# Sums behind the second products, and a group's scatters out of its fourth slot, in a three-attention decoder layer with a routed mixture

## The reference

```python
x = _layernorm(x + _L0_attn_ref(x, ...))            # "ret": scores * decay mask, no softmax, normalised, gated
x = _layernorm(x + _L0_xattn_ref(x, ctx_1024, ...)) # "cross": softmax over the context's rows
h = layernorm(x + self_attention(x), g1, b1)        # "self": causal softmax
probs = softmax(h @ wg); topv, topi = top_k(probs, 2); topv = topv / topv.sum(-1)
h1 = gelu(einsum('bsd,edf->ebsf', h, w1) + bb1)     # 8 experts, 128 -> 512 -> 128
y = einsum('ebsf,efd->ebsd', h1, w2) + bb2
x = _layernorm(x + layernorm(h + moe, g2, b2))      # moe: each row's two experts by their weights
```

## Time and profile before

| | |
|---|---|
| median of three runs | 1313.32 us (1298.87 to 1319.24) |
| profiled execution | 1299.05 us, of which the span from the first to the last instruction is 1297.8 |
| busy in the span | PE 82%, PEld 59%, DVE 67%, ACT 64%, POOL 70% |
| mean granted TensorE clock | 0.893 of full speed |
| longest parts of the chain that ended last | PE 42%, issue 14%, DVE 14%, POOL 14%, ACT 10% |

### The profile page before, as it was taken

The page is one execution under the profiler, slowest core; times in us unless marked ns, Lnnn a source line. Parts: engine busy times, 40 slices in busy tenths (PEclk is TensorE's granted clock), DMA queues, the critical chain, the costliest instruction groups (busy, mean ns, idle before and its releaser), DMA issues.

```text
span 1297.8 us, 45997 instructions
## 1 busy us (share of the span) xinstructions
PE 1063.3 (82%) x17677; PEld 761.5 (59%) x17677; DVE 865.0 (67%) x2370; ACT 824.6 (64%) x1884; POOL 911.1 (70%) x859
## 2 busy tenths in 40 slices
PE   5888888788998888888988888847788799999552
PEld 2555555554555555555555555637777789999310
DVE  4677776766888777777767776545454466666485
ACT  2355554678999887777777776414445466666377
POOL 3788888866766657777777776766666656667596
PEclk9999898987999999989888997657889999999886
DMA  5465332221233223222222221111212233332453
GB/s 158 129 185 147 88 86 63 63 60 54 75 85 85 80 66 85 68 67 68 79 65 65 77 77 35 52 34 43 61 54 63 66 88 98 99 100 78 143 164 97
DMA packets 132181, 108.61 MB, mean 84 GB/s; under 512 B 19563, under 2 KB 122476, under 8 KB 131932
## 3 DMA queue, kind: packets, MB, share of 16 engines
q1 hardware_dynamic: 123548, 88.29, 24.9%
q0 software_dynamic: 8416, 17.38, 3.8%
HBM read 41.58 MB, written 26.75 MB: 53 GB/s over the span
## 4 chain that ended last, share of the span: by engine, by line
PE 42%; issue 14%; DVE 14%; POOL 14%; ACT 10%; DMA 3%; another core or an unknown queue 2%; DVEq 1%; SPq 1%; POOLq 0%; ACTq 0%
PE bank L1211 7%; PE bank L1202 7%; POOL Plo L769 7%; PE bank L547 3%; PE bank L612 3%; PE bank L550 3%; DVE P L841 2%; DMA xrow<-block_rows 2%; PE bank L487 2%; DVE st L873 2%; DVE mx L817 2%; PE bank L450 2%; PE bank L517 2%; PE bank L510 2%
## 5 line engine op out<-in xcount | busy, mean ns | idle before, releaser
L769 POOL TENSOR_TENSOR Plo<-P 128x1024 f16<-128x1024 f32 x192 | 364.7, 1901 | 162.2 <-ACT P L726 136.1
L1254 POOL DMA_INDIRECT expert_rows<-yo,ix x135 | 173.0, 1281 | 103.3 <-DVE ix L1248 73.4
L1225 ACT ACTIVATE G<-bank,we 128x128 f32<-128x128 f32 x540 | 154.9, 372 | 103.6 <-PE bank L1202 85.3
L817 DVE TENSOR_REDUCE mx<-bank 128x16 f16<-128x1024 f32 x128 | 156.7, 1225 | 42.3 <-PE bank L465 33.2
L687 ACT ACTIVATE Kz<-kh,col 128x512 f16<-128x512 f16 x256 | 167.1, 717 | 0.1
L1211 PE MATMUL bank<-we,G 128*128 128x128 f32 x1080 | 151.5, 286 | 16.7 <-ACT G L1225 12.6
L787 POOL DMA_INDIRECT block_rows<-xs,slots x128 | 132.6, 1036 | 39.8 <-issue 38.4
L510 PE MATMUL bank<-Vh,P 64*128 64x17 f16 (+1 forms) x3072 | 148.6, 170 | 10.2 <-issue 10.2
L726 ACT ACTIVATE P<-bank 128x1024 f32<-128x1024 f32 x128 | 131.1, 1024 | 39.7 <-PE bank L487 38.2
L510 PEld LDWEIGHTS bank<-Vh,P 64*128 64x128 bf16 x3072 | 125.6, 94 | 49.8 <-issue 37.2
L511 PE MATMUL bank<-Vh,Plo 64*128 64x17 f16 (+1 forms) x3072 | 145.9, 168 | 9.4 <-issue 9.3
(11 more groups left out here) (187 smaller groups left out, 2169.5 us busy)
## 6 DMA issues: line engine op xcount, KB each, us to landing
Qz<-qh SPq DMA_DIRECT2D x192, 64.0 KB, 2.0
Kst<-kh SPq DMA_DIRECT2D x192, 64.0 KB
xrow<-block_rows SPq DMA_DIRECT2D x135, 65.0 KB
y_t<-expert_rows SPq DMA_DIRECT2D x16, 512.0 KB, 4.1
Qz<-ql SPq DMA_DIRECT2D x96, 64.0 KB, 2.0
Kst<-kl SPq DMA_DIRECT2D x96, 64.0 KB
xT<-xt SPq DMA_DIRECT2D x16, 256.0 KB, 3.1
xs<-x SPq DMA_DIRECT2D x16, 256.0 KB, 4.1
```

The source lines that it names most:

```text
L769: pool.tensor_tensor(Plo[n % 3][:, :], P32[n % 3][:, :], upper(n), ALU.subtract).then_inc(f_Pl.of(n), 1)
L817: dve.tensor_reduce(columns, bank[:, S_BANK:S_BANK + 2, :].rearrange("p r (j i k) -> p r j i k", i=2, k=S), AX_X, ALU.max, negate=True).th ...
L1225: i = act.activation(G[b][:, c, :], bank[:, 2 + p, c * P:(c + 1) * P], ACT.Gelu_apprx_tanh, bias=we[b][:, B1 + c:B1 + c + 1])
L1254: pool.indirect_dma_start(ydst[:, :], bass.IndirectOffsetOnAxis(ix2[s % 4][:, :], 0), yo[s % 4][:, :], None).then_inc(b_sc.of(s), 16)
```

## The change

In slots k = 1, 2 and 3 from slot 117 (GT x ROUTED[0] + 1) to 203, pe_sums is issued as the last thing of the slot, behind pe_router and pe_second. The first slots, k = 0, stay as they are. And where the next routed group is more than one group away, the tiles of a routed group are scattered in slots 2, 4, 5 and 6 behind the start of the group in place of 2, 3, 4 and 5; this holds for i = 0 to 7. Nothing is added or left out.

```diff
-    PLACED = {GT * ROUTED[i + 1] + 2 + t: (i, t) for i in range(NG) for t in range(GT)}
+    PLACED = {}
+    for i in range(NG):
+        apart = i + 2 < len(ROUTED) and ROUTED[i + 2] - ROUTED[i + 1] > 1
+        for t, behind_router in enumerate((2, 4, 5, 6) if apart else (2, 3, 4, 5)):
+            PLACED[GT * ROUTED[i + 1] + behind_router] = (i, t)
...
-        if 0 <= s - LP < TILES:
+        sums_last = k >= 1 and s >= GT * ROUTED[0] and s - LP < TILES
+        if 0 <= s - LP < TILES and not sums_last:
             pe_sums(s - LP)
         if router and s - LP < TILES:
             pe_router(CHOSEN[g])
         pe_second(g, k)
+        if sums_last:
+            pe_sums(s - LP)
```

## The result

The kernel before took 1312.91 us (median of 4 runs), the changed one 1391.55 us (4 runs): ratio 1.067, with a 95% interval of 1.062 to 1.072. The change costs 79 us; the forecast was 1345 us, a cost of about 36 us by its sum. The profiled execution of the changed kernel took 1401.26 us, with a span of 1400.0 us, so it is 102 us longer than the one profiled before. It was the slowest of its four, and the one profiled before was close to the fastest, so this is more than the 79 us of the medians.

The account below looks back on a forecast made before the run. TensorE was taken as the bound, idling 26.8 us ahead of the sums and 20.4 ahead of L593. Terms 20.4 + 10.5 + 9 - 3.5 = +36.4 us gave 1335 (profiled) or 1349 (median); forecast 1345, range 1304 to 1374.

Parts of the forecast that it names:

- Term C: Fourth slots, sums behind the V product: results about 0.5 us later through to L593's wait, 19 groups, +9 us.
- term D: Moved scatters: POOL reaches nmr sooner, -3.5 us; stretched sums only change which ones are hit, 0 us.
- Term A: Second slot of ten routed groups: K product waits for logits behind the later sums, +2.29 us each, +20.4 us.
- Term B: Clock behind the new K product wait: 3.4 us at half clock costs 1.3 us, eight in ten, +10.5 us.
- More sums are hit: Rival: all sums of a longer group meet a scatter, +17, half clock +8: 1360, by the median 1374; chance 0.14.
- The stretching goes: First rival: sums fall between scatters, 26.8 us of idling and half clock go: 1288, by the median 1302; chance 0.20.
- term A alone: Rival: clock doesn't fall after the K product's new wait, fourth-slot delay hidden: 1316, by the median 1330; chance 0.22.

Follow-up runs that it names:

- router_slot_kept: The change, but in slots with the router the sums stay ahead of it; ratio 1.034 to the kernel before.
- fourth_kept: The change, but in the fourth slot the sums stay ahead of the V product; ratio 1.040 to the kernel before.
- pe_only: The kernel before with TensorE's new order of the sums only, scatters in their old slots; ratio 1.059.
- router_slot_alone_filled: The kernel before with sums moved last only in routed groups' second slots, plus three clock-keeping matmuls inside the wait for the logits; ratio 1.018.
- pool_only: The kernel before with only the scatters moved to their new slots, TensorE's order as before; ratio 1.028.
- router_slot_alone_logits_first: The kernel before with sums moved last only in routed groups' second slots, and VectorE copying the router's logits ahead of the results; ratio 1.010.
- first_pair_later: The change with the first scatter pair of a routed group one slot later (3, 4, 5, 6); ratio 1.050 to the kernel before.

## Why the prediction was wrong

The direction was right, and the cost was less than half of what was measured: 36 of 79 us, with the result above the range. Two steps failed most. Term C gave no clock to a wait that it lets arise: 9 us forecast, 29 alone, 33 in the whole. And term D asked only which sums the moved scatters hit, and put them at a gain of 3.5 us; by themselves they cost 33, and 9 on top of the rest. What each part costs in the stretch, moved alone from the kernel before, and what the whole loses when only that part is put back:

| part | forecast us | moved alone us | put back us |
|---|---|---|---|
| A and B, routed second slots | 30.9 | 36 | 41 (router_slot_kept) |
| C, fourth slots | 9 | 29 | 33 (fourth_kept) |
| D, scatters | -3.5 | 33 | 9 (pe_only) |

- **Term A, +20.4 us: right.** The 2.2 us from the sums' end to L551 were measured as 2.21 in group 41, the wait came ten times, and it sums to 16.0 us; by itself the waiting costs about 19 us (router_slot_alone_filled).
- **Term B, +10.5 us: too small.** It gave each wait one stretch of 3.4 us at half clock, eight in ten, 27 us in all. Alone, the waits brought 54 us of half clock, and 17 us of time. The price of a us at half was nearly right: what the stretch lost beyond idling, by the growth of half clock, is 17/54, 23/81 and 19/64 us in the parts alone and 49/143, or 0.34, in the whole, against the 0.38 of the forecast's own 1.3 of 3.4 us. The number of us was wrong, but this term lacks only some 7 us. Of the 143 us of half clock in the whole, putting back A and B takes away 65, C 51 and D 20, so they are no single term's.
- **Term C, +9 us: the wait right, the clock put at nothing.** Filled, the fourth slots alone cost 10 us in the stretch, the forecast's 9. Unfilled they cost 29. The forecast saw that the delay would end in the wait ahead of L593 "for which TensorE waits anyway". In the routed groups 33 to 41 it waited there for 0.3 us at most (0.23 in group 39), so the wait there is new, and the step gave it no clock.
- **Term D, -3.5 us and 0: wrong in sign.** That POOL's nmr would no longer be waited for came true: between 440 and 960 us ACT's L732 waited 16.0 us for it before, L739 waits 2.4 now. But L616 waits 3.2 us where L612 waited 3.7, so nothing was gained. The sums' idling is the same in all (23.3 against 22.0 us), as the net of 0 said. What the step left out is what else stands beside POOL's queue: without the pair between them two Plo run in a row, VectorE's marking lasts until they end, and the maxima of the longer groups come late. L597 waits 16 us more in pool_only, and with the clock behind it the scatters cost 33 us in the stretch. In the whole change the marking lies beside one Plo and takes 1.8 us (2.3 in pe_only), which fits that the scatters add only 9 us there.
- **Not foreseen.** The divisions of the fourth slots that start only 0.7 us behind a scatter pair's end. What they cost by themselves was not separated: fourth_kept removes them together with the rest of term C.
- **The rivals.** "More sums are hit" (1374) is the nearest in time and wrong in mechanism, for the sums' idling didn't grow. "The stretching goes" and "term A alone" are refuted. The prediction says that its range takes in the first rival's middle at 1302, but a range from 1304 leaves it out.

The single terms add up to 36 + 29 + 33 = 98 us in the stretch and the whole to 84. It fits that they share time, as a group that is at half clock already can't lose its clock a second time, but no run shows it. Three things stay open. The sums of the third slots, and of the second slots of groups without the router, were never moved by themselves; pe_only costs 75 us, and terms A, B and C alone 65. How much of D's 33 us hangs on the marking beside Plo isn't known. And it isn't known why 1.0% is left in router_slot_alone_logits_first, where nothing waits for the logits.

## What to carry to other kernels

A stretch that runs at full clock with TensorE nearly always busy is where a new wait is dearest: price the wait and then the slots behind it at half clock (here about 0.3 us for each us at half), not one short stretch. Ask of each delay in which groups the wait that it ends in exists now: the total of 19 us ahead of L593 hides that five of nineteen groups have 0.3 us or less. When an engine's queue changes, look at every instruction beside it on the other engines, and not only at the one that the change was made for. And measure each term by itself, from the kernel before, with a filled twin that keeps the wait and holds the clock: the pair of runs tells waiting and clock apart, which taking parts out of the whole doesn't.

## What the runs showed of the hardware

A wait of 1.3 us ahead of L597 was followed by 8 us at a mean clock of 0.57 with TensorE busy for the whole 8 us; with 0.86 us of it filled the group stayed at 1.00. After an equal wait in group 43 it stayed at 1.00 too. The Trainium skill, page "TensorE: Matmul & The Clock Gate", section "HAM oscillation — how this bites in real kernels", sees the danger in longer idle gaps than this; here the trace differs, for this gap was 1.3 us, and no wait for the logits in the change was over 2.0 us.

Sums that end while a scatter runs can be reported late: L861 started at 747.70, 2.69 us behind their recorded end and 0.70 behind the scatters'. And a VectorE instruction of 64 columns with two inputs in SBUF (L938) took 2885 ns in the mean in pool_only and 190 where no Plo lay beside it. In eight groups it ended 0.1 us behind the second of two POOL instructions that read SBUF; a scatter beside it didn't lengthen it (190 to 200 ns in first_pair_later). The Trainium skill says in "SBUF — State Buffer", section "Who interferes with whom", that such an instruction contends with a GpSimd instruction that reads SBUF; the trace agrees, with 1247 ns in the mean before and 1559 in the change.

```profile
L938 DVE TENSOR_TENSOR chosen<-experts,order_of 128x64 bf16<-128x64 f32 x9 | 14.0, 1559 | 0.0
```
